# Expert weights w1 fetched once per token tile by ScalarE's DMA queue, in place of a fetch per expert and a copy on VectorE

## What is computed

```python
h = feats * rsqrt(deg_out)[:, None]
m = segment_sum(h[src], dst) * rsqrt(deg_in)[:, None]
x = m @ W_gc + b_gc + feats @ W_res + b_res
vals, idx = top_k(x @ Wg + bg, 2);  gates = softmax(vals)
# for each token and each of its two experts e:
h1 = gelu(x @ w1[e] + b1[e])            # w1[e]: 256 x 512, 512 KB
y  = gate * (h1 @ w2[e] + b2[e])        # w2[e]: 512 x 256, 512 KB
core = sum of the two y of a token
z = batchnorm(x + core) * gamma + beta  # over the nodes
out = layernorm(feats + z)
```

## Time and profile before

| | |
|---|---|
| time, median of 3 runs | 1649.5 us (1649.35 to 1653.19) |
| the profiled execution | 1655.46 us |
| its span, first to last instruction | 1653.6 us |
| PE busy | 1483.0 us (90%) |
| DVE busy | 1096.2 us (66%) |
| ACT busy | 697.4 us (42%) |
| POOL busy | 469.6 us (28%) |
| DMA | 188.11 MB, mean 114 GB/s |
| experts' stage: first gather to last scatter | 1043.69 to 1548.71 us |

### The profile page before, as it was taken

How to read it: one execution, slowest core, us unless ns; L and a number is a source line. 1 busy time by engine, 2 the same in 40 slices (tenths; PEclk the granted TensorE clock), 3 DMA queues, 4 the chain that set the end, 5 groups by cost and what they waited for, 6 DMA issues and landing times.

```text
span 1653.6 us, 42138 instructions
## 1 busy us (share of the span) xinstructions
PE 1483.0 (90%) x11682; PEld 1253.0 (76%) x11683; DVE 1096.2 (66%) x2604; ACT 697.4 (42%) x1610; POOL 469.6 (28%) x442
## 2 busy tenths in 40 slices
PE   5988858999999999999999997699999999999662
PEld 4866747877777787777777786688888888888562
DVE  6976898787788788788778775344444444444377
ACT  1647765443434344434443442233333333333257
POOL 4356100112112112111111212455555555555100
PEclk9998979999999999999999998799999999999785
DMA  9212110101101101101101022786667856763594
GB/s 295 80 61 60 58 37 10 43 14 39 51 13 38 51 13 38 51 13 38 37 27 38 20 71 71 230 271 224 214 218 247 270 178 226 251 215 97 186 301 151
DMA packets 146095, 188.11 MB, mean 114 GB/s; under 512 B 16117, under 2 KB 114200, under 8 KB 145763
## 3 DMA queue, kind: packets, MB, share of 16 engines
q1 hardware_dynamic: 126034, 150.59, 27.8%
q0 software_dynamic: 18144, 35.99, 6.8%
q10 hardware_dynamic: 1872, 1.02, 0.2%
HBM read 141.42 MB, written 51.21 MB: 116 GB/s over the span
## 4 chain that ended last, share of the span: by engine, by line
PE 76%; DVE 6%; issue 5%; ACT 4%; DMA 2%; another core or an unknown queue 2%; DVEq 2%; SPq 1%; POOL 0%; ACTq 0%; POOLq 0%
PE banks L1070 32%; PE banks L1176 13%; PE banks L1185 12%; PE banks L1058 9%; PE banks L974 4%; DVE work L1282 3%; PE banks L955 2%; PE banks L1162 1%; ACT counts_r L803 1%; PE banks L1089 1%; DMA big<-ytab 1%; SPq L571 1%; DVE stats L1738 1%; PE banks L1079 1%
## 5 line engine op out<-in xcount | busy, mean ns | idle before, releaser
L1070 PE MATMUL banks<-parts_r,counts_r 128*128 128x512 f32 x2401 | 609.0, 401 | 13.6 <-ACT counts_r L803 12.6
L1070 PEld LDWEIGHTS banks<-parts_r,counts_r 128*128 128x128 f32 x2401 | 437.1, 189 | 107.2 <-issue 22.3
L803 ACT CAST counts_r<-banks 128x784 fp32r<-128x784 f32 x392 | 301.8, 816 | 445.1 <-PE banks L1058 426.4
L1282 DVE TENSOR_TENSOR work<-edge,iota_two 128x1024 bf16<-128x1024 bf16 (+1 forms) x784 | 435.9, 622 | 47.5 <-PE banks L1058 36.0
L637 POOL DMA_INDIRECT lists<-entry,slot x98 | 120.1, 1225 | 735.4 <-DVEq L1541 661.3
L1176 PE MATMUL banks<-work 128*128 128x128 f32 x1984 | 250.9, 280 | 11.7 <-ACT work L862 4.1
L1176 PEld LDWEIGHTS banks<-work 128*128 128x128 f32 x1984 | 233.6, 193 | 25.2 <-issue 17.0
L1185 PE MATMUL banks<-big,work 128*128 x992 | 234.7, 380 | 1.5 <-ACT work L873 1.5
L1652 DVE COPY work<-work 128x1024 f32 x125 | 94.7, 757 | 184.9 <-PE banks L1176 101.3
L1058 PEld LDWEIGHTS banks<-work 128*128 128x128 bf16 x3136 | 152.8, 98 | 71.8 <-issue 70.4
L1058 PE MATMUL banks<-work 128*128 128x98 bf16 x3136 | 184.8, 210 | 17.8 <-DVE work L1282 9.0
(11 more groups left out here) (219 smaller groups left out, 1182.6 us busy)
## 6 DMA issues: line engine op xcount, KB each, us to landing
work<-in_L_gnn_w_dram SPq DMA_DIRECT2D x64, 512.0 KB
big<-in_L_gnn_w_dram SPq DMA_DIRECT2D x64, 512.0 KB
ytab<-zeros SPq DMA_DIRECT2D x11, 1024.0 KB
big<-in_L_gnn_b_dram SPq DMA_DIRECT2D x64, 128.0 KB
restab<-big SPq DMA_DIRECT2D x7, 896.0 KB, 4.0
big<-xtab SPq DMA_DIRECT2D x7, 896.0 KB
res_mem<-restab SPq DMA_DIRECT2D x24, 256.0 KB, 2.9
xtab<-pair_mem SPq DMA_DIRECT2D x24, 256.0 KB, 2.2
```

Of the source, the lines that this page charges most:

```text
L803: nc.scalar.copy(counts[h][:, :, i * WB * WN:(i + 1) * WB * WN].rearrange("p b (h w) -> p h b w", h=2), built_ps[i % 2][:, :, 0:WB * WV // ...
L1070: last = pe.matmul(agg_ps[h], counts[h][:, b, :], parts[:, b, :], start=(b == 0), stop=(b == NB - 1))
L1282: return dve.tensor_tensor(hot, digits.rearrange("p (c t) -> p c t", t=2).unsqueeze(2).to_broadcast([P, c, n, 2]), iota_two[:, 0:n, :].uns ...
```

## The change

w1 leaves SP's loads and the ring of eight. ScalarE now issues a load of w1 for every tile, from DRAM into one of four fixed places (`w1t`), and TensorE reads its stationary operands there. The copy on VectorE is gone, and with it `stage_w1`, `w1_ready` and the waits in it. `w_landed`, which now speaks of w2 and b2 alone, is waited for by ScalarE in `gelu`. ScalarE issues the first four loads ahead of the first `turned`, and in step t the load of tile t+3, behind the gelu of tile t-1, whose layer 1 was the last reader of that place. Its loop has four tiles for eight. The word of a step carries the expert of tile t+3 where it carried that of t+1. SP starts its loads of experts 2 to 7 once the second gather has landed, not the fourth, and behind the experts it waits for the w1 loads too.

```diff
+ASTEP = 4
+W1RING = 4
-        w1s = part(0, RING * K * H).rearrange("p (s k h) -> p s k h", s=RING, k=K)
+        w1t = part(0, W1RING * K * H).rearrange("p (s k h) -> p s k h", s=W1RING, k=K)
-        w1c = [part(T5 + s * K * H, K * H).rearrange("p (k h) -> p k h", k=K) for s in range(2)]
...
             def load_weights(e, s):
-                sp.dma_start(w1s[:, s, :, :], w1[ds(e, 1), :, :].rearrange("e (k p) h -> p (e k) h", p=P)).then_inc(w_in[s], 16)
                 sp.dma_start(w2s[:, s, :, :], ...).then_inc(w_in[s], 16)
                 sp.dma_start(b2s[:, s, :], ...).then_inc(w_in[s], 16)
...
-            sp.wait_ge(xg_in[3], 16)
+            sp.wait_ge(xg_in[1], 16)
...
+            for s in range(W1RING):
+                loaded = sp.to_reg(((n_tiles + (2 * W1RING - 2 - s)) // W1RING) * 16)
+                sp.wait_ge(tiles_ready, 1)
+                sp.wait_ge(w1_in[s], loaded)
             pairs = ytab[0:2 * N, :].rearrange("(n k) d -> n (k d)", k=2)
...
+            def word(t):
+                return act.value_load(tile_i[0:1, 0, ds(t, 1)], min_val=0, max_val=...)
+            def load_w1(s, e):
+                act.dma_start(w1t[:, s % W1RING], w1[ds(e, 1), :, :].rearrange("e (k p) h -> p (e k) h", p=P)).then_inc(w1_in[s % W1RING], 16)
             def gelu(t, s, e):
+                landed = act.to_reg(e + 1)
+                act.wait_ge(tiles_ready, 1)
+                act.wait_ge(w_landed, landed)
                 act.wait_ge(tile_done, t + (RING - 1))
...
+            for t in range(W1RING):
+                load_w1(t, ...)
             turned(0, 0)
             turned(1, 1)
-            with act.Fori(0, TLOOP // RING) as i:
+            with act.Fori(0, TLOOP // ASTEP) as i:
...
                         with act.If(t < last):
-                            e = expert_before(t)
+                            code = word(t)
                             turned(t + 1, s + 1)
-                            gelu(t - 1, s - 1, e)
+                            gelu(t - 1, s - 1, act.snap(code & (NEXP - 1)))
+                            load_w1(s + W1RING - 1, act.snap((code >> EB) & (NEXP - 1)))
...
-            def layer1(t, s):
-                pe.wait_ge(w1_ready, t + 1)
+            def layer1(t, i, s):
+                pe.wait_ge(tiles_ready, 1)
+                pe.wait_ge(w1_in[s % W1RING], i * (16 * RING // W1RING) + (s // W1RING * 16 + 16))
...
-                        m = pe.matmul(hT_ps[s % 2][:, c, :], w1c[s % 2][:, k, c * P:(c + 1) * P], xT[:, s % 2, k, :],
+                        m = pe.matmul(hT_ps[s % 2][:, c, :], w1t[:, s % W1RING, k, c * P:(c + 1) * P], xT[:, s % 2, k, :],
...
-            def stage_w1(t, s, e):
-                ws = dve.snap(e & (RING - 1))
-                landed = dve.to_reg(e + 1)
-                dve.wait_ge(tiles_ready, 1)
-                dve.wait_ge(w_landed, landed)
-                dve.wait_ge(h_done, t + 1)
-                dve.tensor_copy(w1c[s % 2], w1s[:, ds(ws, 1), :, :].rearrange("p s k h -> p (s k) h")).then_inc(w1_ready, 1)
```

More of the change, by code:

```diff
@@ L195, in gnn_kernel @@
               + [result_mem[NFG][:, 0:K * P].rearrange("p (k n) -> p k n", k=K)])
-        assert T5 + 2 * K * H <= AW + OHW and T5 >= AW and (NB + 2) * D <= AW + OHW and NFG // 2 * RW <= NB * D and LT + NSLOT // P * 4 <= NB * 2 * D
+        assert T5 + H <= AW + OHW and T5 >= AW and RING % W1RING == 0 and (NB + 2) * D <= AW + OHW and NFG // 2 * RW <= NB * D and LT + NSLOT // P * 4 <= NB * 2 * D
         NWIN = NWT * P
@@ L360, in gnn_kernel @@
         w_in = [sem(f"w_in{s}") for s in range(RING)]
-        tx_done, tx_ready, w1_ready, h_done, h1_ready, tile_done, y_ready = (
-            sem("tx_done"), sem("tx_ready"), sem("w1_ready"), sem("h_done"), sem("h1_ready"), sem("tile_done"), sem("y_ready"))
+        w1_in = [sem(f"w1_in{s}") for s in range(W1RING)]
+        tx_done, tx_ready, h_done, h1_ready, tile_done, y_ready = (
+            sem("tx_done"), sem("tx_ready"), sem("h_done"), sem("h1_ready"), sem("tile_done"), sem("y_ready"))
         y_in, f_in = [sem(f"y_in{g}") for g in range(NFG + 1)], [sem(f"f_in{g}") for g in range(NFG + 1)]
@@ L874, in gelu @@
                                          bias=b1T[:, k, ds(e, 1)]).then_inc(h1_ready, 1)
+            for t in range(W1RING):
+                load_w1(t, act.snap((act.value_load(tile_i[0:1, 1, t:t + 1], min_val=0, max_val=XMAX) >> TPE.bit_length() - 1) & (NEXP - 1)))
             turned(0, 0)
             turned(1, 1)
-            with act.Fori(0, TLOOP // RING) as i:
-                with act.If(i * RING < last + 1):
-                    for s in range(1, RING + 1):
-                        t = i * RING + s
+            with act.Fori(0, TLOOP // ASTEP) as i:
+                with act.If(i * ASTEP < last + 1):
+                    for s in range(1, ASTEP + 1):
+                        t = i * ASTEP + s
                         with act.If(t < last):
-                            e = expert_before(t)
+                            code = word(t)
                             turned(t + 1, s + 1)
-                            gelu(t - 1, s - 1, e)
+                            gelu(t - 1, s - 1, act.snap(code & (NEXP - 1)))
+                            load_w1(s + W1RING - 1, act.snap((code >> EB) & (NEXP - 1)))
                         with act.Else():
                             with act.If(t < last + 1):
-                                gelu(t - 1, s - 1, expert_before(t))
+                                gelu(t - 1, s - 1, act.snap(word(t) & (NEXP - 1)))
             nc.scalar.preload_act_table(ACT.Sqrt)
@@ L1204, in _ @@
             turn(1, 0, 1)
-            layer1(0, 0)
+            layer1(0, 0, 0)
             with pe.Fori(0, TLOOP // RING) as i:
@@ L1660, in _ @@
             dve.wait_ge(list_in, 16)
-            dve.wait_ge(b1_ready, 1)
             for t in range(AHEAD):
-                x = dve.snap(dve.value_load(tile_i[0:1, 1, t:t + 1], min_val=0, max_val=XMAX))
-                keep_list(x, 0, t)
-                if t in (3, 4):
-                    stage_w1(t - 3, t - 3, dve.snap(dve.value_load(tile_i[0:1, 1, t - 3:t - 2], min_val=0, max_val=XMAX) >> TPE.bit_length() - 1))
+                keep_list(dve.snap(dve.value_load(tile_i[0:1, 1, t:t + 1], min_val=0, max_val=XMAX)), 0, t)
             with dve.Fori(0, TLOOP // RING) as i:
@@ L1672, in _ @@
                             code = dve.value_load(tile_i[0:1, 0, ds(t, 1)], min_val=0, max_val=((XMAX + 1) << 2 * EB) - 1)
-                            with dve.If(t < last):
-                                stage_w1(t + 1, s + 1, dve.snap((code >> EB) & (NEXP - 1)))
                             result(t - 1, s - 1, dve.snap(code & (RING - 1)))
```

15 lines of the change are left out of this document (7 added, 8 removed).

## The result

The changed kernel takes 1628.33 us (median of 4 runs, 1627.96 to 1632.8), the kernel before 1649.88 us (4 runs, 1649.35 to 1653.19). The ratio is 0.9857, interval 0.983 to 0.9884: 21.5 us faster, where 11.8 were forecast, and 3.7 us under the low end of the range.

A forecast was written before the change was run, and what follows sets the result against it. The prediction took the experts' stage to be bound by TensorE, with short gaps. Its terms, -14.5 + 0 + 1.5 + 0.5 + 0.7 = -11.8 us, took 1649.5 to 1637.7 us; range 1632 to 1643, with rivals to 1653.

The forecast's parts named there:

- The copy's wait, -14.5: Experts' stage: in 43 intervals layer 1 starts right behind VectorE's copy; removing the copy gains all 14.5 us.
- New waits for DMA, +1.5: Experts' stage: per-tile w1 loads sometimes land late in fuller DMA queues, costing 1.5 us, bounds 0 and 15.
- 9 us at worst: Longest time for a w1 load beside an x reload, a w2 and a gather, against 10 us of lead.
- The sum of bytes: 63 more w1 loads, 33 MB, raise DMA share from 0.69 to 0.9, the rate from 226 to some 300 GB/s.
- ScalarE, 0: ScalarE's sequencer: load issue and register work, 0.85 us of 2.1 us free per tile, cost nothing.
- rival B: ScalarE's sequencer becomes the bound if an issue takes 1.82 us or more; at 2.1 us, 1664 us; chance 0.06.
- the shorter loop: ScalarE's loop of four tiles passes 31 times for 16; cost 0, bounds 0 to 31 x 0.3 us.
- The start, +0.5: Start of the stage: ScalarE's four first loads delay lists and gathers by 0.5 us, bounds 0 and 2.5.
- The end, +0.7: Behind the last scatter: SP's four more waits for w1 cost 0.7 us, bounds 0.5 and 1.
- A: Rival inside the stage: w1 lands late when the queue is full, price 4 to 12 us, middle 1647; chance 0.13.
- C: Rival: DMA engines become the bound; at only 280 GB/s the period is 4.15 us, total 1670; chance 0.06.
- D: Rival: nothing gained, as another wait of the same length stands behind the copy, 1650 us; chance 0.05.

The follow-up runs named there:

- e1: Kernel before, with VectorE's copy of w1 kept but made two tiles ahead into four places; 1591.58 us, ratio 0.9893 to the kernel before.
- e2: Changed kernel plus an old-size copy on VectorE in each tile that nobody waits for; 1591.3 us, kernel before on that chip 1608.98.
- e12: Changed kernel with an old-size copy, layer 1's wait for it, and the old register work, `w_landed` wait and run-time address put back; 1612.52 us, ratio 1.0028 to before.
- e7: Changed kernel with each load of w1 issued twice, the second into a place nobody reads; 1676.56 us, kernel before on that chip 1605.15.
- e5: Changed kernel with ScalarE's loop over eight tiles in place of four; 1692.56 us, kernel before on that chip 1636.96.
- e3: Kernel before with its copy of w1 cut to a half, the rest not copied; 1617.89 us, kernel before on that chip 1636.96.
- e11: Changed kernel with an old-size copy at the old place, between fixed places, and layer 1 waiting for it; 1599.7 us, ratio 0.995 to the kernel before.

## Why the prediction was right in kind and wrong in size

**The step that failed** is "The shortest tiles, wherever they stand, are 3.81 to 3.84 us, so 3.83 is TensorE's own time." TensorE's own time is 3.735 us. One of the 121 intervals shows it outright, the one behind the layer 1 of 1268.04, which starts without a wait and ends in one of 0.01 us (3.743 us unrounded), against "wherever they stand":

```profile
1268.04 1.95 PE L1176 MATMUL banks<-work 128*128 128x128 f32 x16
...
1271.79 2.05 PE L1176 MATMUL banks<-work 128*128 128x128 f32 x16
```

What looked like one shortest period was two kinds of interval that happen to be nearly as long. In 69 of them the first layer 1 has waited and loads its first weights with nothing to hide them: 3.735 + 0.10 = 3.83. In 51 of the other 52 it hasn't, but the layer 1 at the end waits, in nearly all of them 0.07 us or more: 3.81 and up. So each interval but one had a loss in it, and the shortest of them was no measure of the engine. 121 x 0.095 = 11.5 us were missing, the difference between an excess of 30.4 and the 18.9 us of gaps that were summed: the waits are 20.7 us, not some 15, and the 6.4 us at the restarts were not in the sum at all. The number could have been had from the earlier trace rows: layer 1 to layer 2 where nothing waited (1189.20 to 1190.99) is 1.79 us, layer 2 to the next transposes 1.73 (1187.25 to 1188.98, in the timeline but not among those rows), the transposes 0.22 (to 1189.20); 3.74 in all, each part from where it stood clean. The interval of 3.83 at 1185.37 has 1.88 in the place of 1.79.

**The copy's wait, -14.5.** Right in what it names, and too small by the failed step: against 3.735 us the waits right behind the copy are 20.2 us, and each is followed by its 0.10. Over 3.83 us a tile, 18.9 us were gaps, and 4.8 are left, 4.1 of them at two stops of 5.85 and 5.89 us of which there were two before as well. That the wait is the cause, e1 (the copy kept, the wait gone), e2 (the copy without the wait) and e12 (the wait and what led to it put back) show.

**New waits for DMA, +1.5.** None for w1. The loads end 2.9 to 8.1 us after their issue and have 10, so the prediction's "9 us at worst" was near, and the rate of 301 is under the 375 that the engines give (e7). The sum of bytes came within about 1%. One of the stops has a wait for a gather, 1.0 us.

**ScalarE, 0.** Right for the kernel as it is: of the 121 issues in these tiles the 69 that stand alone take 0.39 us, and at most 0.40; the 52 beside an issue of SP's take 0.47 in the median and at most 0.49. So the rival B, with 1.82, was far off. The Trainium skill, "Perfetto Trace Analysis", section "DMA Instruction — HWDGE (DVE, Sync)", has one DGE block that the DVE and Sync sequencers share, with a wait for a lock; for ScalarE beside SP no more than 0.1 us of such a wait is seen here. But the prediction counted "the shorter loop" at 0 for a wrong reason: it weighed what 31 passes cost for 16 (0.22 us at each branch, beside other work), and not what the body of eight would have cost, 78 us (e5). Four tiles a pass is no side matter; the rest of the change depends on it.

**The start, +0.5.** Layer 1 of tile 0 is 1.2 us later, by the mechanism that was named (the loads ahead of the gathers); 1.0 of it is back by tile 2, since one stop between tiles 0 and 2 is gone. Inside the bounds of 0 and 2.5.

**The end, +0.7.** 0.65 us. Four waits, 0.17 us each.

**Own time and median.** I took the gain of the profiled pair for that of the medians. The stage's 24.3 us stand against 21.5 in the medians, 19.6 and 20.3 on other chips. With the 11.5 us of the failed step the sum would have been -23.3.

**Rivals.** A fell with the missing waits. C was 25% away, and the Trainium skill's rule that queues of different issuers share the same 16 engines ("DMA: Bandwidth & Descriptors", section "Issuing engines are not separate DMA queues") agrees with e7, where a third queue full of work ends at 375 GB/s together. D fell with the first result.

## What to carry to other kernels

Before taking the shortest period in a trace for an engine's own time, look at whether every period has some small loss in it, at its start or at its end, and add up the parts where each stands without one. Here a wait of layer 1 cost its length, of which the first 0.16 us didn't show as idle, and then 0.10 us more. Look at how long a chain must be to be just late: moving the work a tile earlier (e1) gave nearly what removing it gave, and halving it (e3) gave most of that. When instructions are added to a loop's body, ask whether the body still stays on the engine, and look for an instruction queue in the stage.

## What was not expected of the hardware

- A layer 1 that waited, however briefly, took 0.10 us more, and the first 0.16 us of its wait lay under the records of the transposes. The profile counts both as busy: 13.8 us less busy time after the change, for the same 3149 matmul records.
- With eight tiles in ScalarE's loop it stood 3.2 to 6.0 us behind the loop's branch, for 0.22 us with four, and there were five packets of 8 KB for a pass on an instruction queue. TensorE, idle for 3.5 us by it, then ran its next layer 2 in 3.65 us for 1.89, at a granted clock of 0.53 (e5).
- Three queues together moved 375 GB/s over 400 us (e7).
- A load of 512 KB took 2.9 to 8.1 us from its issue to its last packet in the changed kernel, 5.0 in the median, three times the 1.6 us that its bytes alone were reckoned at.
- 0.45 us of register work and waits ahead of a copy, with a copy 0.08 us longer, made 12.8 us over 121 tiles (e11 and e12).
